# One fused attention and expert block on one NeuronCore: the last half's third norm by way of VectorE, its gates over four PSUM banks, and a new order at the end

## What is computed

```
x = x + layernorm(attn(layernorm(x)))        # attn has a residual of its own: n + ripple(n)
x = x + layernorm(ffn(layernorm(x)))
```

```
scores = sigmoid(x @ gate_W) * route_scale
topk_scores, topk_idx = top_k(scores, 2)
h = gelu(x @ W1 + b1);  y = h @ W2 + b2
out = sum_e(gate_e * y_e) + gelu(x @ Ws1 + bs1) @ Ws2 + bs2
```

## Time and profile before

| | us |
|---|---|
| median of 3 runs (300.3 to 300.32) | 300.31 |
| the profiled execution's own time | 298.65 |
| its span in the profile | 296.9 |

### The profile page before, as it was taken

One profiled execution on the slowest core, in us unless ns is written; L12 is line 12 of the kernel. 1 busy time (PEld: TensorE's weight loads), 2 busy tenths in 40 slices (PEclk: granted clock), 3 DMA queues, 4 the chain that ended last, 5 costly groups with the idle time before them and its releaser, 6 DMA issues.

```text
span 296.9 us, 4788 instructions
## 1 busy us (share of the span) xinstructions
PE 250.2 (84%) x1639; PEld 173.5 (58%) x1639; DVE 245.5 (83%) x570; ACT 198.4 (67%) x461; POOL 110.9 (37%) x161
## 2 busy tenths in 40 slices
PE   5849909887699899989898899989898697699893
PEld 5424605776165467678546486777555485584383
DVE  6699989988997699799896899799957997727743
ACT  3476655447879956898499746989597253476841
POOL 5967699522434004025471104046530141230023
PEclk9998977999799999999999999999999999999999
DMA  7527602003989730308999601019899301000003
GB/s 202 129 78 216 195 0 72 2 0 62 235 244 202 172 71 0 108 0 164 253 236 234 127 9 38 0 27 226 265 218 217 71 3 35 0 3 1 0 13 95
DMA packets 22963, 31.34 MB, mean 106 GB/s; under 512 B 3909, under 2 KB 17054, under 8 KB 22938
## 3 DMA queue, kind: packets, MB, share of 16 engines
q1 hardware_dynamic: 20346, 21.59, 25.6%
q0 software_dynamic: 2592, 9.44, 17.5%
HBM read 5.07 MB, written 2.10 MB: 24 GB/s over the span
## 4 chain that ended last, share of the span: by engine, by line
PE 41%; DVE 31%; ACT 18%; issue 5%; POOL 4%; POOLq 0%; DVEq 0%; ACTq 0%
DVE prods L1026 7%; DVE prods L283 5%; PE psH L1356 5%; PE psY L1459 4%; PE psF L1421 3%; PE psG L1459 3%; PE psA L1459 3%; PE psA L1252 3%; DVE hid L1137 3%; PE psA L1324 2%; ACT xn L718 2%; PE psF L1396 2%; ACT xn L598 2%; DVE den L997 2%; PE psY L1303 2%
## 5 line engine op out<-in xcount | busy, mean ns | idle before, releaser
L474 POOL TENSOR_SCALAR var<-ss 128x4 f32<-128x4 f32 (+1 forms) x25 | 13.5, 539 | 105.8 <-ACT squares L764 51.6
L283 DVE TENSOR_TENSOR prods<-qT,kT 128x1024 f32<-128x1024 f32 (+1 forms) x44 | 50.9, 1212 | 2.2 <-ACT qT L587 2.2
L1356 PE MATMUL psH<-ident,prods 128*128 128x128 f32 x324 | 40.1, 273 | 0.0
L1356 PEld LDWEIGHTS psH<-ident,prods 128*128 128x128 f32 x324 | 36.4, 141 | 2.3 <-issue 2.3
L1026 DVE TENSOR_TENSOR prods<-v_shift,prob 128x896 f32<-128x896 f32 x32 | 35.7, 1115 | 0.0
L1137 DVE TENSOR_TENSOR hid<-hid,psG 128x512 f32<-128x512 f32 x32 | 20.8, 683 | 15.8 <-PE psG L1445 15.2
L476 POOL TENSOR_TENSOR rstd<-var,neg_half 128x4 f32<-128x4 f32 (+2 forms) x28 | 31.8, 1137 | 2.3
L1324 PE MATMUL psA<-prods,slot_sel 128*32 128x512 f32 x168 | 26.1, 677 | 6.1 <-DVE prods L283 5.9
L1421 PE MATMUL psF<-x3T,w 128*128 128x512 f32 x58 | 29.0, 610 | 0.4 <-ACT gexp L732 0.3
L1026 DVE TENSOR_TENSOR prods<-v_tok,prob 128x128 f32<-128x128 f32 (+2 forms) x60 | 25.5, 450 | 0.0
L495 POOL DMA_DIRECT2D convT<-tapT x9 | 8.2, 913 | 43.4 <-DMA convT<-tapT 24.6
(11 more groups left out here) (237 smaller groups left out, 612.1 us busy)
## 6 DMA issues: line engine op xcount, KB each, us to landing
v_shift<-v_tok SPq DMA_DIRECT2D x20, 448.0 KB
convT<-tapT POOLq DMA_DIRECT2D x9, 512.0 KB, 4.9
x_res<-L_attn_x SPq DMA_DIRECT2D x4, 512.0 KB, 9.6
out<-y_out SPq DMA_DIRECT2D x7, 256.0 KB, 2.3
x_in<-L_attn_x SPq DMA_DIRECT2D x3, 512.0 KB, 4.1
v_shift<-v_tok SPq DMA_DIRECT2D x4, 384.0 KB
tapT<-tapT POOLq DMA_DIRECT2D x3, 512.0 KB, 9.8
convT<-kexp POOLq DMA_DIRECT2D x3, 512.0 KB, 7.5
```

Of the source, the lines that this page charges most:

```text
L283: return eng.tensor_tensor(prods[:, QUADS * (s % 2) + q, t0:t1], qT[:, t0:t1], kT[:, PRE - off + t0:PRE - off + t1], ALU.mult)
L474: nc.gpsimd.tensor_scalar(var[:, cols], src, scale, EPS, ALU.mult, ALU.add).then_inc(step, 1)
L1356: ins = pe.matmul(dst, terms[:, j % TERM_BUFS, m, :], ident[:], is_transpose=True, start=False, stop=(m == live[-1]))
```

## The change

It touches the turn b = 3 at its end and the turn b = 4, that is units 5, 6 and 7.

- **DVE**: `residual` of unit 6 stands before the multiplications of tile 7 instead of behind them. For unit 7 the variance of the third norm comes from what is there already: x2 - mean = (x - mean) + y x rstd2, and y sums to zero over a row, so var3 = var1 + rstd2 x (2/P sum(x y) + rstd2 x ss2 / P) + eps. `last_variance` forms the cross sum tile by tile from `psH` and `x_res` and then does four steps on 128x4 elements; `last_normalise` writes xn3 of unit 7 on DVE.
- **POOL**: `ln3(7)`, three instructions, becomes one power in `last_ln3`.
- **ACT**: `norm3_squares(7)` and `normalise3(7)` are gone. `normalise3(6)` stands before `norm2(7)`. The gelus of unit 6's chunks 0 and 1 stand before the copy of its turned gates.
- **PE**: unit 5's four tiles of `experts_out` are spread over the front of units 6 and 7, in the place of two of the three fillers. Unit 6's tile 0 stands before the turn of unit 7's gates, its tile 1 behind it, and its tiles 2 and 3 behind the four spreads of unit 7, of which chunks 2 and 3 go to the two banks of `psF`.

```diff
+        def spread_bank(u, c):
+            return psF[:, 3 - c, :] if u == 2 * B - 1 and c >= 2 else psG[:, c % 2, :]
...
+            def last_ln3():
+                pool.wait_ge(last_var, 1)
+                nc.gpsimd.tensor_tensor(rstd3[:, TPH:NT], var3[:, TPH:NT], neg_half[:, TPH:NT],
+                                        ALU.pow).then_inc(last_rstd, 1)
...
                 if not attn:
-                    ln3(u1)
+                    last_ln3()
...
                         nc.scalar.activation(table_load[:], neg_half[:, 0:1], ACT.Exp)
+                        normalise3(2 * b)
                         norm2(2 * b + 1)
-                        normalise3(2 * b)
...
                     evacuate_x3(u0)
-                    norm3_squares(u1)
                     gate_logits(u0)
-                    normalise3(u1)
                     evacuate_x3(u1)
                     gate_logits(u1)
                     shared_hidden(u0)
+                    hidden(u0, range(0, 2))
                     gates_expert_major(u0)
-                    hidden(u0, range(0, 4))
+                    hidden(u0, range(2, 4))
...
+            def last_variance():
+                u, tiles = 2 * B - 1, slice(TPH, NT)
+                scratch = tapT[0][:, 0:HALF].rearrange("p (j c) -> p j c", c=P)
+                dve.wait_ge(ss2_ready, u + 1)
+                dve.wait_ge(x_res_ld, upto(u // 2, N_DMA, N_DMA))
+                last_chain.start(dve, 0)
+                for n, j in enumerate(range(TPH, NT)):
+                    ins = nc.vector.scalar_tensor_tensor(out=scratch[:, n, :], in0=attended(1)[:, bass.ts(n, P)], scalar=2.0 / P,
+                                                         in1=x_res[:, j, :], op0=ALU.mult, op1=ALU.mult,
+                                                         accum_out=cross[:, n:n + 1])
+                last_chain(ins)
+                dve.wait_ge(ln2_ready, u + 1)
+                last_chain(nc.vector.scalar_tensor_tensor(out=var3[:, tiles], in0=ss2[:, tiles], scalar=1.0 / P,
+                                                          in1=rstd2[:, tiles], op0=ALU.mult, op1=ALU.mult))
+                last_chain(nc.vector.tensor_tensor(var3[:, tiles], var3[:, tiles], cross[:], ALU.add))
+                last_chain(nc.vector.tensor_tensor(var3[:, tiles], var3[:, tiles], rstd2[:, tiles], ALU.mult))
+                nc.vector.scalar_tensor_tensor(out=var3[:, tiles], in0=var3[:, tiles], scalar=EPS,
+                                               in1=mv[:, tiles, 1], op0=ALU.add, op1=ALU.add).then_inc(last_var, 1)
+
+            def last_normalise():
+                u = 2 * B - 1
+                dve.wait_ge(last_rstd, 1)
+                dve.wait_ge(x2_ready, upto(u, TPH, TPH))
+                for j in range(TPH, NT):
+                    last = nc.vector.tensor_scalar(xn3[:, j, :], x2_of(u)[:, j, :], neg_mean[:, u // 2 % 3, j:j + 1],
+                                                   rstd3[:, j:j + 1], ALU.add, ALU.mult)
+                last.then_inc(last_xn3, 1)
...
-                    nc.vector.tensor_tensor(hid[:, c, cols], hid[:, c, cols], psG[:, c % 2, :],
+                    nc.vector.tensor_tensor(hid[:, c, cols], hid[:, c, cols], spread_bank(u, c),
...
+                if not attn:
+                    last_variance()
                 if ffn:
                     residual(u1)
+                if not attn:
+                    last_normalise()
...
+                        if j == NT - 1 and not more:
+                            residual(2 * b)
                         weigh(b, j, two_gate_steps)
...
-                    residual(2 * b)
+                    if more:
+                        residual(2 * b)
                     add_conv(b, 1)
...
-                    if c >= 2 or u == 2 * B - 1:
+                    if u == 2 * B - 1 and c >= 2:
+                        pe.wait_ge(hidden_free, upto(u, N_HIDDEN, 2 * c - 2))
+                    elif c >= 2 or u == 2 * B - 1:
                         pe.wait_ge(gated, upto(u, 4, c - 1))
-                    pe.matmul(psG[:, c % 2, :], gate_sel[:, c, :], gT[:, u % 2, :], start=True, stop=True).then_inc(gate_spread, 1)
+                    pe.matmul(spread_bank(u, c), gate_sel[:, c, :], gT[:, u % 2, :], start=True, stop=True).then_inc(gate_spread, 1)
...
-                    if ffn:
-                        experts_out(u1, range(TPH if more else TPH - 1))
+                    if ffn and more:
+                        experts_out(u1)
```

More of the change, by code:

```diff
@@ L73 @@
 N_GATE_STEPS = 24
+N_LAST_STEPS = 4
 LAST_BANKS = (0, 1, 2, 3, 0, 1, 2, 0)
@@ L206, in block_kernel @@
         gtmp = [sb(f"gtmp{i}", [P, TPH, EXPERTS]) for i in range(10)]
+        cross = sb("cross", [P, TPH])
         gmax = [sb(f"gmax{i}", [P, TPH]) for i in range(6)]
@@ L253, in block_kernel @@
         gate_step, gT_ready, experts_summed = sem("gate_step"), sem("gT_ready"), sem("experts_summed")
+        last_step, last_var, last_rstd, last_xn3 = sem("last_step"), sem("last_var"), sem("last_rstd"), sem("last_xn3")
         ss4_ready, out_scaled = sem("ss4_ready"), sem("out_scaled")
         out_ready = [sem(f"out_ready{h}") for h in range(2)]
+        last_chain = Chain(last_step, N_LAST_STEPS)
         softmax_chain = Chain(softmax_step, N_SOFTMAX_STEPS)
@@ L1384, in turn_x3 @@
                     keep_busy(FILL_X3, front(u, X3))
-                pe.wait_ge(xn3_ready, u + 1)
+                if u == 2 * B - 1:
+                    pe.wait_ge(last_xn3, 1)
+                else:
+                    pe.wait_ge(xn3_ready, u + 1)
                 for n, j in enumerate(unit_tiles(u)):
@@ L1550, in _ @@
                     turn_x3(u0)
-                    experts_out(u0 - 1, range(TPH - 1, TPH))
+                    experts_out(u0 - 1, range(0, 1))
                     gate_logits(u0)
-                    keep_busy(FILL_FRONT, spare)
+                    experts_out(u0 - 1, range(1, 2))
                     turn_logits(u0)
+                    experts_out(u0 - 1, range(2, 3))
                     hidden(u0, range(0, 2))
@@ L1558, in _ @@
                     gate_logits(u1)
-                    keep_busy(FILL_FRONT, spare)
+                    experts_out(u0 - 1, range(3, TPH))
                     turn_logits(u1)
@@ L1568, in _ @@
                     hidden(u1, range(2, 4))
+                    experts_out(u0, (0,))
                     gates_expert_major(u1)
-                    experts_out(u0, (0,))
-                    spread_gates(u1, range(0, 2))
                     experts_out(u0, (1,))
-                    spread_gates(u1, (2,))
-                    experts_out(u0, (2,))
-                    spread_gates(u1, (3,))
-                    experts_out(u0, (3,))
+                    spread_gates(u1, range(0, 4))
+                    experts_out(u0, range(2, TPH))
                     experts_out(u1)
```

## The result

The changed kernel takes **301.5 us** (median of 20 runs, 300.73 to 303.0) against 300.31 us (20 runs of the kernel before, 298.81 to 303.25). The ratio is 1.0045, with a 95% interval of 1.0029 to 1.0061: slower by 0.45%, where 299.65 us and a range up to 300.7 us were forecast. The profiled execution took 301.03 us with a span of 299.2 us and a mean granted clock of 0.963, against 0.977.

The account below looks back on a forecast made before the run. Bound by DVE and PE waiting for each other, then a relay of PE, ACT, POOL and DVE, then 16 us of PE alone. -0.19 - 0.45 = -0.64 took 300.31 to 299.65 us; range 298.9 to 300.7.

Parts of the forecast that it names:

- the clock falls: Behind the turn of unit 6's gates, PE idles 1.9 us and its clock falls about 3 us: 301.3 us; chance 0.10.
- Step 1: Unit 6's residual ahead of tile 7's multiplications on DVE: the convolution's sum comes 0.52 us later.
- Step 2: Front of unit 6: its gexp about 2.1 us earlier, with `evacuate_x3(6)` at 261.28 instead of 263.50.
- Step 3: Unit 7's xn3 made by DVE: hidden, ready between 265.9 and 267.1, before PE's `turn_x3(7)` at 267.43.
- Step 4: Front of unit 7: its gexp 1.4 us earlier, 271.29 instead of 272.68.
- Step 5: ACT's copy of unit 6's gates, behind two gelus: 0.2 us earlier, `hidden(7)` at 276.09 instead of 276.28.
- Step 6: PE's last 16 us, from `hidden(7)` on: 0.45 us less, through spreads in a row and tiles no longer parted.
- rival of a larger gain: Cheaper tiles, hidden products and gelus make the front 0.5 us shorter: -1.15, 299.15 us; chance 0.18.
- rival in which DVE is held: POOL's power for unit 6 holds DVE's multiplication of tile 7: all that follows 1.0 later, +0.4, 300.7 us; chance 0.04.

## Why the prediction was wrong

**The step that failed** is the rival "the clock falls", held at 0.10. It had the place (behind the turn of unit 6's gates), the length of the idle (1.9 forecast, 1.83 measured) and the sign right, and the sum left it out. By the mean granted clock it happened in most executions if not in all: all 20 lie between 0.948 and 0.963. With the idle filled 9 of 12 lie at 0.968 to 0.975, and 6.8 us at half clock are 0.011 of the mean. The mean alone can't tell this fall from another, and 5 of the 24 executions of the kernel before that were taken beside that run lie under 0.963 as well.

Its chance came from a wrong match. I set the gap against turn 3's, where an idle of 1.89 had kept the clock, and took turn 1's for a microsecond, since I read it off one stage of 1 us; it was 1.75 us long, and the clock had fallen behind it. So the trace had both outcomes for an idle of this length, which a chance of 0.10 does not say. The prediction also had it that what decides is how busy the engine was ahead of the gap. With the fillers behind the gap PE's work ahead of it is that of the changed kernel, and the clock stayed, so what follows counts; no run varied what stands ahead.

It was mis-sized too: I priced it from turn 1's fall, put at 3 us long (3.4 measured) and 1.6 us dear; it was 6.8 us long and cost 3.22 us of tail (46.64 less 43.42). That the rival's 301.3 us lies near the measured 301.5 is luck: by the tails the change with the fall is 2.19 dearer, not the 0.96 of that sum, and the scatter between the profiled executions and the medians makes up the rest. The Trainium skill (TensorE: Matmul & The Clock Gate, What's actually happening) says that the gate follows how busy the engine has been of late and knows two levels; on the levels the trace agrees, with 1.00 and 0.50 and values between only where a stage holds both.

**The other steps held**, by the table of the tail and the runs:

- Step 1, forecast +0.52 for the convolution's sum: 257.97 less the 0.11 by which the profiles are apart is 257.86 against 257.35, so +0.51.
- Step 2, `evacuate_x3(6)` 2.2 us earlier: 2.25. Taking back the residual's move lost 1.39 us, so steps 1 and 2 together are worth it.
- Step 3, hidden: xn3(7) was written by 265.98, and PE came for it at 267.54, or 267.43 on the clock of the kernel before (forecast 265.9 to 267.1, and 267.43). That the second agrees to the hundredth is luck: two tiles took 1.21 each and not 1.15, the product of the logits began 0.08 late, and four records of `hidden(6)` took 1.73 and not 1.90. And the first thing that the step's 1.29 us are worth is ACT's free time, which step 2 counted without saying that it hung on this step.
- Step 4, 1.4: 1.35. Step 5, 0.2: 0.19 at the copy. Both are within 0.05.
- Step 6, forecast 0.45: 0.63 alone in the kernel before. The tile between `hidden(7)` and the turn of the gates costs 1.21 and not 1.31, which I had not counted (0.10), and the wait for DVE was 0.15 and not 0.05.
- With the clock kept the whole change is worth 1.03 of tail, where I had summed 0.64. That is near the -1.15 of the rival of a larger gain, but not for its reason: the front was 0.21 shorter at the spread, as forecast. Of the rest, 0.18 is at `hidden(7)`: it starts 0.53 behind the spread (276.30 to 276.83) instead of 0.71, since its bank had been freed by the gelus that now stand ahead. That is the one good thing about their new place.

Last, whether DVE and POOL hold each other up. The changed kernel's DVE (the third line is the normalisation of unit 7, done at 265.98), then its POOL:

```profile
255.26 1.08 DVE L1038 TENSOR_TENSOR prods<-v_shift,prob 128x896 f32<-128x896 f32 x1
256.26 1.28 DVE L1179 TENSOR_TENSOR hid<-hid,psG 128x512 f32<-128x512 f32 x2
...
264.87 1.11 DVE L1098 TENSOR_SCALAR xn<-qexp,neg_mean,rstd 128x128 f32<-128x128 f32 x4
...
255.67 0.73 POOL L482 TENSOR_SCALAR var<-ss 128x4 f32<-128x4 f32 x1 [2.83 <-ACT squares L724]
256.48 1.01 POOL L484 TENSOR_TENSOR rstd<-var,neg_half 128x4 f32<-128x4 f32 x1
```

POOL's step, 0.19 when alone, took 0.73 beside DVE's multiplication, which took its usual 1.08; POOL's power then ran beside `gate_hidden`, which took its usual 1.28. The Trainium skill (SBUF — State Buffer, Who interferes with whom) would have the first pair exclude each other and leave the second alone, as VectorE has one input in SBUF there: by that rule the trace agrees. Four us earlier it did not go by that rule, as the prediction had seen in the kernel before: two DVE multiplications with both inputs in SBUF began at 251.84, 0.01 behind a power of POOL of 1.02 us, and took 0.79 together for their usual 0.75. The rival in which DVE is held did not come about.

## What to carry to other kernels

When an edit lengthens an idle stretch of TensorE, price the clock before anything else: collect every stretch of about that length in the same trace, with its length read from the timeline and not from a stage, see at which of them the clock fell, and try the edit with fillers in it, which here turned a kernel that was 0.45% slower into one that is no slower than before. Work put ahead of a small copy that another engine waits for was paid twice here: 1.12 us as delay, and 3.22 us by the clock that the longer idle brought down. Here the copy ahead of the two gelus brought 297.6 us, 0.7% under the kernel before; of the versions run, that one and the one with unit 5's tile moved (297.0 us) are the fastest, and the profiles don't tell them apart.

## What the runs showed of the hardware that I had not expected

- An idle of 1.83 us cost 6.8 us of half clock, and the fall came 1.4 us after PE had work again (matmuls from 275.47, clock 0.50 from 276.9). The same 1.83 us, with fourteen transposes 0.53 us behind its end, kept the clock at 1.00.
- In one profiled execution each, an idle of 0.81 us at this place kept the clock and one of 1.25 us lost it for 3.4 us. An idle of 2.79 us in turn 3 was kept in some executions and not in others, in the same code.
- The four cross sums of 128x128 with an accumulator start 0.21 us apart on DVE (0.91 us for all, 261.52 to 262.43), though each brings a read of its accumulator of 0.08 us; four residuals of the same size hold DVE for 1.04, 0.26 each. I had taken at least a residual's time for them.
